# G from three fp32r products instead of one fp32 product, with cur2 and x split in high and low parts

## The reference

```python
for W in (f0, f1, f2):                               # f0: (39*39, 128), f1, f2: (128*39, 128)
    z = einsum('bfd,bgd->bfgd', x0, xk).reshape(b, f * g, d)
    xk = einsum('bpd,pm->bmd', z, W); outs.append(xk)
z = sum(concatenate(outs, axis=1), axis=-1)          # (1024, 384)
h = concatenate([z, dense_ctx], axis=1)
h = maximum(h @ W_top1 + b_top1, 0); h = maximum(h @ W_top2 + b_top2, 0)
y = h @ W_top3
```

## Time and profile before

| | us |
|---|---|
| median of 3 runs | 1282.8 |
| profiled execution | 1282.42 |
| its span | 1280.6 |
| TensorE products (PE) busy | 1243.7 (97%) |
| VectorE (DVE) busy | 1052.2 (82%) |
| ScalarE (ACT) busy | 952.7 (74%) |
| GpSimd (POOL) busy | 955.7 (75%) |

### The profile page before, as it was taken

One profiled execution on the slowest core, in us unless ns is written; L12 is line 12 of the kernel. 1 busy time (PEld: TensorE's weight loads), 2 busy tenths in 40 slices (PEclk: granted clock), 3 DMA queues, 4 the chain that ended last, 5 costly groups with the idle time before them and its releaser, 6 DMA issues. The chain is left out here.

```text
span 1280.6 us, 21991 instructions
## 1 busy us (share of the span) xinstructions
PE 1243.7 (97%) x5919; PEld 1010.2 (79%) x5919; DVE 1052.2 (82%) x3208; ACT 952.7 (74%) x3115; POOL 955.7 (75%) x743
## 2 busy tenths in 40 slices
PE   3699999999999999999999999999999999999998
PEld 2477778888788887888878888788878888888887
DVE  3499999788987899788897799978899788988873
ACT  2488888678876788678886788867888678877772
POOL 7588888678886888767886778867888678874461
PEclk9899999999999999999999999999999999999999
DMA  6474334331333332323333133332233332232000
GB/s 154 106 208 84 79 82 82 80 69 44 69 74 79 80 71 58 71 53 83 82 78 74 29 70 83 83 79 56 45 73 79 81 80 59 59 67 67 4 1 1
DMA packets 137182, 92.02 MB, mean 72 GB/s; under 512 B 92355, under 2 KB 100035, under 8 KB 136718
## 3 DMA queue, kind: packets, MB, share of 16 engines
q1 hardware_dynamic: 126819, 87.99, 30.0%
q0 software_dynamic: 10240, 2.64, 2.6%
HBM read 84.08 MB, written 3.87 MB: 69 GB/s over the span
## 5 line engine op out<-in xcount | busy, mean ns | idle before, releaser
L423 ACT ACTIVATE parts<-pieces,x_cols 128x128 f32<-128x128 f32 x2560 | 728.1, 373 | 236.1 <-PE pieces L746 179.5
L571 DVE SCALAR_TENSOR_TENSOR parts<-pieces,x_cols,parts 128x128 f32<-128x128 f32 x2432 | 685.5, 345 | 180.6 <-PE pieces L746 133.5
L744 PE MATMUL pieces<-w_hi,cur_hi 128*128 128x512 f32 (+1 forms) x1280 | 543.0, 424 | 9.8 <-issue 6.2
L746 PE MATMUL pieces<-w_hi,cur_lo 128*128 128x512 f32 (+1 forms) x1280 | 498.7, 390 | 0.0
L745 PE MATMUL pieces<-w_lo,cur_hi 128*128 128x512 f32 (+1 forms) x1280 | 498.6, 390 | 0.0
L372 POOL TENSOR_TENSOR parts<-parts 128x1024 f32<-128x1024 f32 x127 | 304.7, 2400 | 184.9 <-DVE parts L571 180.2
L363 POOL DMA_INDIRECT emb<-in_table,rows x320 | 312.6, 977 | 81.9 <-issue 67.3
L744 PEld LDWEIGHTS pieces<-w_hi,cur_hi 128*128 128x128 f32 x1280 | 241.7, 189 | 68.4 <-issue 10.7
L746 PEld LDWEIGHTS pieces<-w_hi,cur_lo 128*128 128x128 f32 x1280 | 241.0, 188 | 51.8
L745 PEld LDWEIGHTS pieces<-w_lo,cur_hi 128*128 128x128 f32 x1280 | 241.9, 189 | 50.7
L377 POOL TENSOR_TENSOR tails<-parts 128x512 f32<-128x512 f32 x127 | 164.3, 1294 | 18.1
(11 more groups left out here) (81 smaller groups left out, 633.6 us busy)
## 6 DMA issues: line engine op xcount, KB each, us to landing
partners<-x_wide SPq DMA_DIRECT2D x93, 468.0 KB
x_end<-x_wide SPq DMA_DIRECT2D x96, 80.0 KB
x_rep<-x_wide SPq DMA_DIRECT2D x96, 78.0 KB
partners<-x_wide SPq DMA_DIRECT2D x93, 80.0 KB
emb<-in_table,rows POOLq DMA_INDIRECT x320
x_diag<-x_cols SPq DMA_DIRECT2D x256, 10.0 KB
partners<-x_wide SPq DMA_DIRECT2D x31, 132.0 KB
x_wide<-emb SPq DMA_DIRECT2D x32, 80.0 KB
```

The costliest lines, as they stand in the source:

```text
L423: last = nc.scalar.activation(parts[n % 2][:, 4 * i + r, :], src[:, r * H:(r + 1) * H], ACT.Copy, scale=x_cols[n // 4][:, n % 4, f:f + 1])
L571: nc.vector.scalar_tensor_tensor(acc, src[:, r * H:(r + 1) * H], x_cols[n // 4][:, n % 4, f:f + 1], acc, ALU.mult, ALU.add).then_inc(acc_d ...
L744: nc.tensor.matmul(dst[:, 0:width], hi[:, cols], w1_hi[:, ws], start=True, stop=False)
L746: nc.tensor.matmul(dst[:, 0:width], lo[:, cols], w1_hi[:, ws], start=False, stop=True).then_inc(l2d_ready if q in D_PIECES else l2a_ready, 1)
```

## The change

`cur2` (now two buffers) is split: ScalarE copies it to fp32r (`take_cur2_high`, step 9 of the second block behind), VectorE subtracts that from it (`take_cur2_low`, step 0 of the third block behind); `cur2_hi` and `cur2_lo` have three buffers each. x_cols of a tile is split in the same way into `x_split`, at steps 20 and 22 of the tile before. `make_g` makes three fp32r products of 320 columns: high × high, high × low of x, low × high. It stands two steps later (10n+34, and 4, 14, 24 in place of 2, 12, 22; the first four of a quad stay). An `x_diag` buffer now holds high and low parts of two blocks instead of four blocks. `load_diag` runs twice a tile, 8 transfers each, for the same tile: the first half between `store_tile` and `load_x` of the tile two ahead, the second behind `load_partners`. Half 0 waits for the second G of the tile before, half 1 for the fourth.

```diff
 G_LAG = 3
-G_STEP = {10 * n + 32: (0, n) for n in range(4, BLOCKS - G_LAG)}
-G_STEP.update({49: (0, 0), 53: (0, 1), 60: (0, 2), 64: (0, 3), 2: (1, 13), 12: (1, 14), 22: (1, 15)})
+G_STEP = {10 * n + 34: (0, n) for n in range(4, BLOCKS - G_LAG)}
+G_STEP.update({49: (0, 0), 53: (0, 1), 60: (0, 2), 64: (0, 3), 4: (1, 13), 14: (1, 14), 24: (1, 15)})
...
 S_Y = 159
-Q_HALVE, Q_FINISH = 7, 8
+Q_HALVE, Q_FINISH, Q_HIGH, Q_LOW = 7, 8, 9, 0
+S_X_HIGH, S_X_LOW = 20, 22
 CURS = 3
...
         tails = [sb(f"tails{i}", [P, 4, H]) for i in range(2)]
-        cur2 = [sb(f"cur2_{i}", [P, H]) for i in range(CURS)]
-        x_diag = [sb(f"x_diag{i}", [P, 4, BLK_B, FX]) for i in range(2)]
+        cur2 = [sb(f"cur2_{i}", [P, H]) for i in range(2)]
+        cur2_hi = [sb(f"cur2_hi{i}", [P, H], F32R) for i in range(CURS)]
+        cur2_lo = [sb(f"cur2_lo{i}", [P, H], F32R) for i in range(CURS)]
+        x_split = [sb(f"x_split{i}", [P, 4, 2, FX], F32R) for i in range(2)]
+        x_diag = [sb(f"x_diag{i}", [P, 2, 2, BLK_B, FX], F32R) for i in range(2)]
         G = sb("G", [P, TILES, FX, TILE_B])
...
-            def load_diag(tile, i):
-                turned, used = value(sp, tile + 1), value(sp, (tile - 1) * 4)
-                sp.wait_ge(x_cols_ready, turned)
-                wait(sp, g_ready, used)
+            def load_diag(tile, i, half):
+                split, used = value(sp, tile + 1), value(sp, (tile - 1) * 4 + 2 * half + 2)
+                sp.wait_ge(x_lo_ready, split)
+                if not isinstance(tile, int) or tile > 0:
+                    sp.wait_ge(g_ready, used)
                 for b in range(BLK_B):
                     at = slice(b * D, (b + 1) * D)
-                    sp.dma_start(x_diag[i % 2][at, :, b, :], x_cols[i][at]).then_inc(x_diag_loaded[i % 2], 16)
+                    sp.dma_start(x_diag[half][at, :, :, b, :].bitcast(FP32), x_split[i % 2][at, 2 * half:2 * half + 2].bitcast(FP32)
+                                 ).then_inc(x_diag_loaded[half], 16)
...
             sp.wait_ge(diag_cleared, 2)
-            load_diag(0, 0)
             def quad(u, first, last):
...
                     if ahead:
                         store_tile(tile + 2, (i + 2) % TILES)
+                    load_diag(tile, i, 0)
+                    if ahead:
                         load_x(tile + 2, (i + 2) % TILES)
                         load_partners(tile + 2, (i + 2) % TILES)
-                    if not (last and i == TILES - 1):
-                        load_diag(tile + 1, (i + 1) % TILES)
+                    load_diag(tile, i, 1)
                     if first and i == 0:
...
                 wait(act, acc_done, (tile - 3) * 4 * D_OPS)
-                if i >= 2:
-                    wait(act, x_diag_loaded[i % 2], (tile - i) // 2 * 16 * DIAG_LOADS)
-                else:
-                    wait(act, x_diag_loaded[i % 2], (tile - i - 2) // 2 * 16 * DIAG_LOADS)
                 src = gx_bank[:, X_AT:X_AT + 4 * F].rearrange("p (j f) -> p j f", f=F)
                 nc.scalar.activation(x_cols[i][:, :, 0:F], src, ACT.Copy).then_inc(x_cols_ready, 1)
+            def take_x_high(tile, i):
+                act.wait_ge(x_cols_ready, tile + 1)
+                for half in range(2):
+                    wait(act, x_diag_loaded[half], (tile - 1) * 16 * DIAG_LOADS)
+                nc.scalar.activation(x_split[i % 2][:, :, 0, :], x_cols[i][:], ACT.Copy).then_inc(x_hi_ready, 1)
+            def take_cur2_high(u, n):
+                g = u * BLOCKS + n
+                act.wait_ge(cur2_ready, g + 1)
+                wait(act, g_ready, g - CURS + 1)
+                nc.scalar.activation(cur2_hi[g % CURS][:], cur2[n % 2][:], ACT.Copy).then_inc(cur2_hi_ready, 1)
             def copy_x_rep(tile, i):
...
                             copy_x_cols(tile + 1, (i + 1) % TILES)
+                        if more and s == S_X_HIGH:
+                            take_x_high(tile + 1, (i + 1) % TILES)
+                        if q == Q_HIGH:
+                            if n >= 2:
+                                take_cur2_high(u, n - 2)
+                            elif not first:
+                                take_cur2_high(u - 1, BLOCKS + n - 2)
                         if at - 1 in G_STEP:
...
             u = QUADS - 1
-            for n in range(BLOCKS - G_LAG, BLOCKS):
+            copy_g(u, BLOCKS - 3)
+            for n in range(BLOCKS - 2, BLOCKS):
+                take_cur2_high(u, n)
                 copy_g(u, n)
...
             def finish_cur2(u, n):
                 g, v = u * BLOCKS + n, tails[n % 2]
+                wait(dve, cur2_lo_ready, g - 1)
+                dve.wait_ge(halved, g + 1)
+                nc.vector.tensor_tensor(cur2[n % 2][:], v[:, 0], v[:, 1], ALU.add).then_inc(cur2_ready, 1)
+            def take_cur2_low(u, n):
+                g = u * BLOCKS + n
+                dve.wait_ge(cur2_hi_ready, g + 1)
                 wait(dve, g_ready, g - CURS + 1)
-                dve.wait_ge(halved, g + 1)
-                nc.vector.tensor_tensor(cur2[g % CURS][:], v[:, 0], v[:, 1], ALU.add).then_inc(cur2_ready, 1)
+                nc.vector.tensor_tensor(cur2_lo[g % CURS][:], cur2[n % 2][:], cur2_hi[g % CURS][:].bitcast(FP32),
+                                        ALU.subtract).then_inc(cur2_lo_ready, 1)
+            def take_x_low(tile, i):
+                dve.wait_ge(x_hi_ready, tile + 1)
+                nc.vector.tensor_tensor(x_split[i % 2][:, :, 1, :], x_cols[i][:],
+                                        x_split[i % 2][:, :, 0, :].bitcast(FP32), ALU.subtract).then_inc(x_lo_ready, 1)
...
             take_cur1(0, 0, 0)
+            take_x_low(0, 0)
             def quad(u, first, last):
...
                             take_pairs_low(tile + 1, i + 1, S_LOW.index(s))
+                        if q == Q_LOW:
+                            if n >= 3:
+                                take_cur2_low(u, n - 3)
+                            elif not first:
+                                take_cur2_low(u - 1, BLOCKS + n - 3)
+                        if more and s == S_X_LOW:
+                            take_x_low(tile + 1, (i + 1) % TILES)
                         if more and s == S_SUM[-1] + 2:
...
             over_quads(dve, quad)
+            take_cur2_low(QUADS - 1, BLOCKS - 3)
             halve_tails(QUADS - 1, BLOCKS - 2)
...
             add_last_parts()
+            take_cur2_low(QUADS - 1, BLOCKS - 2)
             halve_tails(QUADS - 1, BLOCKS - 1)
             finish_cur2(QUADS - 1, BLOCKS - 1)
+            take_cur2_low(QUADS - 1, BLOCKS - 1)
...
             def make_g(u, n, turned=QUADS * TILES):
                 g = u * BLOCKS + n
-                pe.wait_ge(cur2_ready, g + 1)
+                pe.wait_ge(cur2_lo_ready, g + 1)
                 pe.wait_ge(x_cols_ready, turned)
-                if n % 4 == 0:
+                if n % 2 == 0:
                     tile = u * TILES + n // 4
-                    pe.wait_ge(x_diag_loaded[n // 4 % 2], (tile - n // 4 % 2) * 8 * DIAG_LOADS + 16 * DIAG_LOADS)
+                    pe.wait_ge(x_diag_loaded[n // 2 % 2], (tile + 1) * 16 * DIAG_LOADS)
                 wait(pe, g_copied, g)
-                nc.tensor.matmul(gx_bank[:, 0:FX * BLK_B], cur2[g % CURS][:],
-                                 x_diag[n // 4 % 2][:, n % 4].rearrange("p b f -> p (b f)"),
-                                 start=True, stop=True).then_inc(g_ready, 1)
+                dst, hi, lo = gx_bank[:, 0:FX * BLK_B], cur2_hi[g % CURS][:], cur2_lo[g % CURS][:]
+                x_hi, x_lo = [x_diag[n // 2 % 2][:, n % 2, e].rearrange("p b f -> p (b f)") for e in range(2)]
+                nc.tensor.matmul(dst, hi, x_hi, start=True, stop=False)
+                nc.tensor.matmul(dst, hi, x_lo, start=False, stop=False)
+                nc.tensor.matmul(dst, lo, x_hi, start=False, stop=True).then_inc(g_ready, 1)
             def layer3(u, step, tiles):
```

More of the change, by code:

```diff
@@ L215, in cin_kernel @@
         cur2_ready = sem("cur2_ready")
+        cur2_hi_ready = sem("cur2_hi_ready")
+        cur2_lo_ready = sem("cur2_lo_ready")
+        x_hi_ready = sem("x_hi_ready")
+        x_lo_ready = sem("x_lo_ready")
         diag_cleared = sem("diag_cleared")
@@ L387, in _ @@
             for i in range(2):
-                pool.memset(x_diag[i][:], 0.0).then_inc(diag_cleared, 1)
+                pool.memset(x_diag[i][:].bitcast(FP32), 0.0).then_inc(diag_cleared, 1)
             find_rows(2, 2)
@@ L511, in _ @@
             copy_cur1_hi(0, 0)
+            take_x_high(0, 0)
             act.wait_ge(w1_lo_ready, 2)
```

## The result

The changed kernel takes 1422.7 us (median of 5; 1418.37 to 1423.56) against 1282.8: 1.1085 times the time before, 95% interval 1.107 to 1.1099. 1273 us was forecast, 10 us faster; it is 140 us slower.

A forecast was written before the change was run, and what follows sets the result against it. TensorE's issue was taken as the bound from about 60 us to the last piece. −12.0 (G) + 0 + 0 + 2.2 (tail) = −9.8 us, giving 1273.0 us from a median of 1282.8; range 1269.5 to 1278.

The forecast's parts named there:

- VectorE and ScalarE: Added copies and subtractions: 0.20 us each per block, 0.25 per tile, 1.05 us more per tile, costed at 0.
- The G product: Two fp32 records replaced by three fp32r products of 0.147 us: 0.096 us saved per G, 12.0 us over 125.
- the rivals with 0.136 and with 0.189: Shorter products, 0.136 us each: 1268.9 us, chance 0.05; products held to weight loads of 0.189 us: 1289 us, 0.03.
- Cover: VectorE's and ScalarE's idle places absorb the added operations: cost 0, with 0 to 0.4 us a tile as ends.
- The first rival: VectorE sets the pace in the pair stretch, nothing absorbed: 0.85 us a tile, 26 us, 1299 us; chance 0.03.
- the half case: VectorE's additions in the pair stretch partly exposed, 0.4 us a tile: 1285 us; chance 0.05.
- The point from which it decides: VectorE as the pace was to decide once the lost time passes 0.35 us a tile.
- Transfers: x_diag doubled to 16 transfers a tile, load_x 18 us later in a quad's second tile, nine microseconds' cover: cost 0.
- The start: Engines stand still from 45.5 to 51.6, then half clock up to 60; costed at 0, with −2 to +3 us.
- a sign of being wrong: The prediction called itself wrong if, among other signs, the pause at the kernel's beginning moves.
- The tail: G of block 14 waits for its low part behind add_last_parts, delaying G of block 15: +2.2 us.
- a rival at 0.08: TensorE's pause near the kernel's end lowers the clock, layer 3 partly at half rate, 2 to 4 us: 1276; chance 0.08.

The follow-up runs named there:

- the pair that prices it: Changed kernel without VectorE subtractions, three fp32r products for G, 1272.8 us, against the same with one fp32 product, 1283.7 us.
- the SBUF twin: Changed kernel with the cur2_low subtraction moved into step 1's piece, beside GpSimd's first add, both operands in SBUF: 1358.9 us.

## Why the prediction was wrong

The step that failed is, under *VectorE and ScalarE*, "so a queue loses 0.20 us to it". I priced the subtraction by L641, the instruction most like it in shape, and put it at another step. Measured: 1.63 us in the mean at step 0, that is 2.12 to 2.20 us in 91 of 128 blocks and 0.28 to 0.29 in the others; x_low, taken at 0.25, has 1.21. L641 stands at step 8, where GpSimd's adds are over; step 0 is where they begin. The cause is shown from both sides: the subtraction alone brings 100 us into the kernel before, a PSUM operand takes the clash away at the same place, and another place, or an add that waits, takes it away with the same operands.

The Trainium skill has the rule, and I did not weigh it: SBUF — State Buffer, SBUF: two separate sides, says that VectorE and GpSimd share a pair of ports as an exclusive lock, which a VectorE instruction with two SBUF inputs takes against a GpSimd instruction that reads SBUF; whichever starts first holds it for the whole instruction. The runs agree: 2.12 to 2.20 us where the add is first, with the end 0.15 us behind the add's, and 0.28 us where VectorE is. That GpSimd is held when VectorE is first shows too. In the changed kernel x_low starts once 0.04 us ahead of an add; it keeps its 0.32 us, and the add takes 1.43 us, where the mean is 1.28:

```profile
70.90 0.32 DVE L681 TENSOR_TENSOR x_split<-x_cols,x_split 128x160 fp32r<-128x160 f32 x1
```

```profile
70.94 1.43 POOL L384 TENSOR_TENSOR parts<-parts 128x512 f32<-128x512 f32 x1
```

GpSimd's subtraction takes 452 to 485 ns ahead of the adds, where no such instruction of VectorE meets it, and up to 781 behind them, where halves do (ns, min/median/max, the first and the second of the two kernels with low parts on GpSimd):

```profile
L383 POOL TENSOR_TENSOR cur_lo<-cur,cur_hi x125: 452/463/485, 79.8 to 1247.6; 128x128 fp32r<-128x128 f32 x125
```

```profile
L390 POOL TENSOR_TENSOR cur_lo<-cur,cur_hi x125: 452/464/781, 82.7 to 1244.9; 128x128 fp32r<-128x128 f32 x125
```

The trace of before had a row on it. Durations of the halves (ns, min/median/max), VectorE's records at the longest of them and GpSimd's:

```profile
L635 DVE TENSOR_TENSOR tails<-tails x128: 410/417/1417, 77.7 to 1259.5; 128x256 f32<-128x256 f32 x128
```

```profile
91.53 0.68 DVE L603 TENSOR_TENSOR pairs_lo<-pairs,pairs_hi 128x512 fp32r<-128x512 f32 x1
...
93.16 1.42 DVE L635 TENSOR_TENSOR tails<-tails 128x256 f32<-128x256 f32 x1
```

```profile
91.57 1.29 POOL L374 TENSOR_TENSOR parts<-parts 128x512 f32<-128x512 f32 x1
93.00 1.29 POOL L377 TENSOR_TENSOR tails<-parts 128x512 f32<-128x512 f32 x1
```

124 of the 128 halves meet no add, and three begin in the last 0.01 us of one. The one that stands inside an add, at 93.16, takes 1.42 us and ends 0.29 us after the add of 93.00, while L603 at 91.53, with one operand in PSUM, keeps its 0.68 us beside another. A median hides this, a maximum of three times the median shows it.

The other steps:

- *The G product.* 0.441 us for three was taken, 0.44 is measured, so 0.147 a product; the rivals with 0.136 and with 0.189 fall. 12.0 us over 125 was forecast, 10.9 us is the difference of the pair that prices it (8.7 by the ratios).
- *Cover.* "VectorE drains its queue between these stretches" holds for about 0.20 us a block (1273.2 us, as without subtractions) and not for 0.45 (15 us lost). With 1.3 us a block and 0.9 us a tile, 6.2 us a tile, 5.6 us of a 34.8 us tile came through, and 17.5 us of the 25 us of a quad.
- *The first rival* had the engine right (VectorE as the pace) and the price wrong: it took 0.85 us a tile, 1299 us. It was given 0.03, the half case 0.05. The point from which it decides, given as 0.35 us a tile, is 9.8 / 31 = 0.32.
- *Transfers.* No cost, as forecast.
- *The start.* No cost can be told. Its pause did move, which had been named as a sign of being wrong: TensorE's longest idle time there is 6.2 us before and 3.9 us after, and between 2.9 and 10.9 us in the kernels told here. What sets it stays open.
- *The tail.* The 2.2 us pause came and cost 2.6 us. What was a rival at 0.08 came with it, a clock near 1.2 GHz, and added 1.6 us. The rival had it over some 4 us of layer 3, a length that no row shows; it lay ahead of layer 3.

## What to carry to other kernels

Before an instruction is put beside others, ask what the second engine does at that step: the price of an instruction belongs to its place as well as its shape. A VectorE instruction with two operands in SBUF goes where GpSimd isn't adding, gets one operand from PSUM, or goes to GpSimd itself. A mean of the record hides whether it was held in some blocks and not in others; the minimum and the maximum tell. Where an engine is 9.84 of 9.97 us busy in a stretch, 0.2 us more may be covered and 0.45 not.

## What the runs showed that I had not expected

The pause in the tail doesn't always bring the low clock. Six of the kernels told here have it, TensorE idle for 1.96 to 2.22 us before G of block 14. In four the granted clock of the 4 us behind it reads 0.57 to 0.69 (the changed kernel, the one in which GpSimd waits, the one with the PSUM operand, the one with low parts ahead of the adds). In two it stays at 1.00 (the SBUF twin, and the one with x_low at step 28). Of this last one:

```profile
1259.18 0.41 PE L813 MATMUL gx_bank<-x_diag,cur_hi 128*128 128x320 f32 x1 [2.21 <-DVE cur_lo L677]
```

```profile
1259.18:1263.18 4.00, 4.00 (x27) 3.62 (x27) 0.86 (x3) 0.64 (x2) 0.00 (x0) 1.00 0.00 0
```

```profile
1262.67 0.31 PE L813 MATMUL gx_bank<-x_diag,cur_hi 128*128 128x320 f32 x1
```

There G of block 15 follows 3.49 us behind G of block 14, against 5.12 in the changed kernel; what decides between the two stays open. In the start of the kernel before, half clock followed a pause of 6.1 us.

GpSimd needs 463 ns in the median for the 128x128 subtraction for which VectorE needs 281 alone. Even so the kernel with GpSimd's subtractions behind its adds takes 1276.2 us, 3 us more than the fastest one, which has them on VectorE at step 8.
